# Scoring two steps of a narrow block in one pair of PSUM banks: steps 2 with 3 and 4 with 5 become pairs in a float32 decoder layer

## The chip, the cores and the metric

The kernel runs on one core of a Trainium2 chip, as one program. The metric is device time in microseconds (us). A profile is one execution of it, recorded by the hardware profiler; its times are read from the start of its span. TensorE is PE in the views (its weight loads PEld), VectorE is DVE, ScalarE is ACT, GpSimd is POOL and SyncE is SP.

## The reference: what is computed

One layer on x of 4 sequences x 512 tokens x 128 channels, all float32: causal self-attention with 16 heads of 8 channels and a learned relative bias, then cross-attention to 77 context tokens, then a mixture of 8 experts with one shared expert. Only the first part is touched, and the layer norm between the first and the second:

```
x = x + attn(_layernorm(x))
#   logits = where(j <= i, (q.k + q.rel_key[clip(j - i + 255, 0, 255)]) * scale, -inf)
#   out    = softmax(logits) @ v;   out @ Wo + bo
x = x + xattn(_layernorm(x), ctx)
#   q and k are normed once more inside each head
x = x + ffn(_layernorm(x))
```

## The kernel before, in words

Self-attention runs over the 4 sequences b, each in 4 blocks of 128 queries. `ORDER` is [2, 1, 3, 0]: the n-th block of a sequence is query block 2, 1, 3, 0. A block is numbered g = 4b + n, from 0 to 15. Query block 0 sees up to 128 keys and query block 1 up to 256: these are the narrow blocks (n = 3 and n = 1). Blocks 2 and 3 are the wide ones. A block has 8 steps u = 0 to 7 of 16 queries; s = 8g + u counts all 128 steps. A step's rows are 16 queries x 8 heads on 128 partitions, twice: `half` 0 and 1 are two sets of 8 heads in two PSUM banks. `psS` has four banks, and step s uses banks 2(s%2) and 2(s%2)+1.

Each engine's program is written out by hand in one loop over s, and engines meet only at semaphores:

- TensorE: `scores(s)` (L1403: q.k, 16 matmul instructions, and L1413: the relative part, 16 more), then `transpose_weights(s - 2)` (L1432: turns the softmax weights of the step before last), then at u = 2 to 5 `attend_block(g - 1, u - 2)` (L1372: a quarter of the previous block's weighted sum of values). Small things hang on certain steps: `sum_rows` at u = 4 (L1460), `project_o` at u = 7 (L1379), pieces for the cross-attention in the upper half of bank `psM` (`key_piece` L1480, `tokens_piece` L1488, `queries_piece` L1496, `heads_piece` L1504), and `early_probe` (L1513).
- VectorE: the negated maxima of the step's rows (L1058), then the copies of transposed weights of step s - 2 (`copy_units`, L1014), then a piece of a layer norm where there is one. At u = 2 `spread_sums` (L1020, L1021) and at u = 6 `finish` (L990) stand ahead of the maxima.
- ScalarE: some copies of step s - 2 (L625, wide blocks only), then two exponentials of step s (L663), then at u = 5 `copy_inverses` (L610), then the copy of a piece (L631 keys, L637 and L642 tokens and queries, L648 heads).
- GpSimd: `build_queries` makes the masked queries of a block (L479, L485) in one of two slots as soon as the block that used the slot has its scores; between them stand the root of a variance (L445) and `prepare` (L470).

The waits that matter: `scores(s)` waits until the exponentials of step s - 2 have read their banks; the exponentials of s wait for the maxima of s; `transpose_weights(s)` waits for the exponentials of s and, unit by unit, for the copy that empties its `psT` bank; a piece waits for the copy of the piece before it.

The layer norm of sequence f = b - 1 is spread over block n = 1 of the next sequence, as `ln_mean` (L850, L851) at u = 1, `ln_subtract` (L856) at u = 2, `ln_square` (L866) at u = 3, `ln_sum` (L875, L876) at u = 4, and at u = 5 `refine` (L834 to L836, after GpSimd's root) and `ln_multiply` (L888). `tokens_piece` at u = 6 waits for it. The head norm of the queries has its `head_sum` (L920, L921) at u = 7 of n = 2.

Of the kernel before, what the change touches and what calls it, by code (L numbers as in the profile page):

```python
# [60 lines left out]
def build(nc, x, ctx_in, pack_a, pack_b, rel_base, out):  # L61
# [6 lines left out]
    with ExitStack() as stack:  # L68
# [43 lines left out]
        neg_max = sb("neg_max", [128, 2, 2])  # L112
# [146 lines left out]

        def units(blk):  # L260


            return [list(range(j, min(j + 2, blk + 1))) for j in range(0, blk + 1, 2)]
# [62 lines left out]
        KEY_STEPS = (1, 3, 5, 6)  # L326
# [240 lines left out]
        def _(act):  # L567
# [83 lines left out]
            for s in range(ALL_STEPS):  # L651
                g, u = divmod(s, BS)
                b, n = divmod(g, TB)
                wide = width(ORDER[n], u)
                if s >= 2:
                    copy_units(s - 2)
                act.wait_ge(max_ready, s + 1)
# [4 lines left out]
                for half in range(2):  # L662
                    ins = nc.scalar.activation(prob[:, s % 4, half, 0:wide], psS[:, 2 * (s % 2) + half, 0:wide],  # L663
                                               ACT.Exp, bias=neg_max[:, s % 2, half:half + 1],
                                               accum_out=row_sum[:, g % 2, 2 * u + half:2 * u + half + 1])
                ins.then_inc(scores_read, 1)
                if g and u == 5:
# [136 lines left out]
        def _(dve):  # L804
# [240 lines left out]

            for s in range(ALL_STEPS):
                g, u = divmod(s, BS)
                wide = width(ORDER[g % TB], u)
# [6 lines left out]
                if g > 1 and u == 0:  # L1055
                    add_y(g - 2, tile_of(g - 2))
                dve.wait_ge(scores_ready, s + 1)
                v.tensor_reduce(neg_max[:, s % 2], psS[:, 2 * (s % 2):2 * (s % 2) + 2, 0:wide],  # L1058
                                AX_X, ALU.max, negate=True).then_inc(max_ready, 1)
                if s >= 2:  # L1060
                    copy_units(s - 2)
                if s == KEYS_AT:
# [261 lines left out]
        def _(pe):  # L1324
# [62 lines left out]
            def scores(s):  # L1387
# [4 lines left out]
                wide = width(blk, u)  # L1392
# [3 lines left out]
                pe.wait_ge(scores_read, PRO + s - 1)  # L1396


                for c in range(QG // QT):
                    q0 = QG * u + QT * c  # L1400
                    for half in range(2):
                        rows = slice(HALF_ROWS * half, HALF_ROWS * (half + 1))
                        mm(psS[32 * c:32 * c + 32, 2 * (s % 2) + half, 0:wide],  # L1403
# [3 lines left out]
                for c in range(QG // QT):  # L1407
# [493 lines left out]
```

## Time and profile before

| what | value |
|---|---|
| median of 3 runs | 498.47 us (497.95 to 498.8) |
| the profiled execution | 497.16 us, span 495.4 us |
| TensorE (PE) busy | 449.7 us, 91% of the span |
| VectorE (DVE) busy | 335.2 us, 68% |
| ScalarE (ACT) busy | 267.2 us, 54% |
| GpSimd (POOL) busy | 162.0 us, 33% |
| mean granted TensorE clock | 0.976 |
| the 128 steps of self-attention | 36.9 to 338.6 us |

The operations of VectorE in block 5, mean of one: maxima over 2x208 elements 0.59 us (L1058), over 2x160 0.49 us; copy of 512 elements 0.69 us and of 256 elements 0.41 us (L1014; two of 256 per step in query block 1, issued 0.33 us apart); L850, L856, L866, L875 and L888 0.67 to 0.69 us each; L851 and L876 0.17 us; L1020 0.25 us and L1021 0.42 us.

How to read it: busy time is a mean over stages, so what a change is worth is read in its own stretch. A matmul's end is modelled and reaches past the next one's start, so TensorE's phases are read from start to next start. "Idle before" names what released an instruction. PEclk is the granted clock, where 1.00 is 2.4 GHz and 0.50 is 1.2 GHz.

### The profile page before, as it was taken

To read this page: it belongs to the slowest core of one execution; us is meant where nothing else is said; L and a number is where in the kernel's file an instruction comes from. 1 tells how busy PE (TensorE), PEld (TensorE's weight loads), DVE (VectorE), ACT (ScalarE), POOL (GpSimd) and SP (SyncE) were. 2 spreads that over 40 slices of the span, in tenths; PEclk is the share of its full clock that TensorE was granted. 3 is DMA by queue.
4 is the path that set the end of the run, shared out by engine and by line. 5 is a ranking of instruction groups with operands and counts; after the bars stand their busy time and mean duration, and the time that the engine had idled before them with its cause. 6 is when DMAs were issued, how large, how long until landed. Compare 5 with 4: busy or idle time off the path is not lost.

```text
span 495.4 us, 17255 instructions
## 1 busy us (share of the span) xinstructions
PE 449.7 (91%) x7304; PEld 274.2 (55%) x7304; DVE 335.2 (68%) x684; ACT 267.2 (54%) x811; POOL 162.0 (33%) x95
## 2 busy tenths in 40 slices
PE   0879999999999799999799999998898989999997
PEld 0554655655655555655565665564454434666765
DVE  5555886657977667885857887766667587466633
ACT  2546556756456446556535655554454556554653
POOL 7147383333350952360752422084300000001000
PEclk9999999999999799999889999999889899999999
DMA  8211000000100000000000000000000004503151
GB/s 287 66 70 46 26 3 24 24 18 8 26 24 1 24 10 17 26 24 2 24 3 24 3 3 3 3 4 2 2 0 1 1 0 172 171 23 141 53 176 38
DMA packets 17465, 19.49 MB, mean 39 GB/s; under 512 B 1659, under 2 KB 14575, under 8 KB 17263
## 3 DMA queue, kind: packets, MB, share of 16 engines
q1 hardware_dynamic: 17391, 18.41, 11.5%
q8 instruction: 58, 0.95, 0.8%
q14 instruction: 16, 0.13, 0.1%
HBM read 16.17 MB, written 2.16 MB: 37 GB/s over the span
## 4 chain that ended last, share of the span: by engine, by line
PE 70%; DVE 17%; issue 5%; ACT 5%; DMA 2%; POOL 1%; DVEq 0%; SPq 0%; ACTq 0%; POOLq 0%
PE psT L1432 15%; PE psS L1403 14%; PE psS L1413 8%; PE psOM L1372 8%; PE psT L1792 5%; PE psS L1775 4%; DVE neg_max L1058 3%; DVE x_max L1033 2%; PE psS L1622 2%; PE psOM L1513 2%; ACT prob L663 2%; PE psT L1513 2%; PE psOM L1649 1%; DVE prob L1278 1%; PE psOM L1460 1%
## 5 line engine op out<-in xcount | busy, mean ns | idle before, releaser
L663 ACT ACTIVATE prob<-psS,neg_max 128x208 f32<-128x208 f32 (+23 forms) x256 | 121.2, 479 | 74.3 <-DVE neg_max L1058 74.1
L1058 DVE TENSOR_REDUCE neg_max<-psS 128x2 f32<-128x672 f32 (+23 forms) x128 | 91.7, 717 | 64.8 <-PE psS L1413 63.8
L445 POOL TENSOR_TENSOR stat<-stat,pack_a_sb 128x4 f32<-128x4 f32 (+2 forms) x16 | 54.7, 3416 | 169.9 <-DVE stat L876 123.0
L1432 PE MATMUL psT<-pack_a_sb,prob 128*128 128x128 f32 (+4 forms) x640 | 99.2, 287 | 6.3 <-DVE pt_even L1014 3.3
L1432 PEld LDWEIGHTS psT<-pack_a_sb,prob 128*128 128x128 f32 (+4 forms) x640 | 65.1, 133 | 48.5 <-issue 31.4
L1403 PE MATMUL psS<-k_v,q_both 64*32 64x336 f32 (+23 forms) x2048 | 88.5, 403 | 2.6 <-ACT prob L663 1.3
L1413 PE MATMUL psS<-rel_shifted,q_both 36*32 36x268 f32 (+16 forms) x2048 | 71.8, 338 | 0.0
L479 POOL TENSOR_TENSOR q_both<-qT,pack_a_sb 128x1024 f32<-128x1024 f32 x16 | 31.6, 1973 | 85.4 <-PE psS L1413 82.9
L1413 PEld LDWEIGHTS psS<-rel_shifted,q_both 36*32 36x32 f32 x2048 | 37.4, 110 | 24.7 <-issue 17.5
L663 ACT ACTIVATION_READ_ACCUMULATOR prob<-psS,neg_max 128x1 f32 x256 | 50.5, 197 | 0.0
L1792 PEld LDWEIGHTS psT<-pack_b_sb,prob 128*128 128x128 f32 x288 | 36.1, 191 | 18.6 <-DVE prob L1278 11.7
L1014 DVE COPY pt_even<-psT 128x512 f32<-128x512 f32 x64 | 43.6, 682 | 3.4 <-PE psT L1432 3.2
L713 ACT ACTIVATE prob<-psS 77x2048 f32<-77x2048 f32 x16 | 29.9, 1872 | 22.4 <-PE psS L1622 22.4
L1792 PE MATMUL psT<-pack_b_sb,prob 128*128 128x128 f32 x288 | 38.7, 278 | 3.6 <-DVE prob L1278 3.6
L485 POOL TENSOR_TENSOR q_both<-q_rep,pack_a_sb 128x1024 f32<-128x1024 f32 x16 | 41.1, 2568 | 0.0
L1403 PEld LDWEIGHTS psS<-k_v,q_both 64*32 64x32 f32 x2048 | 23.6, 106 | 25.3 <-issue 17.8
L1775 PE MATMUL psS<-qT,pack_b_sb 128*128 128x512 f32 x72 | 36.4, 594 | 0.0
L625 ACT ACTIVATE pt_diag<-psT 80x256 f32<-80x256 f32 (+2 forms) x64 | 23.9, 374 | 23.0 <-PE psT L1432 23.0
L625 ACT ACTIVATE pt_even<-psT 128x256 f32<-128x256 f32 x32 | 12.3, 383 | 33.4 <-PE psT L1432 33.4
L768 ACT ACTIVATE prob<-psS 128x512 f32<-128x512 f32 x36 | 21.2, 590 | 12.2 <-PE psS L1775 12.2
L1014 DVE COPY pt_diag<-psT 80x256 f32<-80x256 f32 (+2 forms) x64 | 26.3, 411 | 0.8 <-PE psT L1432 0.7
L1372 PE MATMUL psOM<-pt_diag,V_now 128*32 128x128 f32 x512 | 26.0, 280 | 0.0
(172 smaller groups left out, 597.7 us busy)
## 6 DMA issues: line engine op xcount, KB each, us to landing
q_rep<-q_scratch SPq DMA_DIRECT2D x128, 32.0 KB
k_v<-w_scratch SPq DMA_DIRECT2D x8, 512.0 KB, 5.9
q_both<-w_scratch SPq DMA_DIRECT2D x8, 512.0 KB, 6.6
pack_b_sb<-pack_b_dram SPq DMA_DIRECT2D x1, 1641.5 KB, 9.7
X<-x_dram SPq DMA_DIRECT2D x4, 256.0 KB, 5.3
q_scratch<-qT SPq DMA_DIRECT2D x4, 256.0 KB, 2.0
out_dram<-X SPq DMA_DIRECT2D x4, 256.0 KB, 2.3
pack_a_sb<-pack_a_dram SPq DMA_DIRECT2D x1, 535.0 KB, 4.4
```

The lines of the kernel that those rows point to most:

```text
L445: nc.gpsimd.tensor_tensor(st[:, 5, 0:groups], st[:, 2, 0:groups], ca["root"][0:parts, 0:groups], ALU.pow).then_inc(seeded, 1)
L485: nc.gpsimd.tensor_tensor(q_rel[:, slot].rearrange("p (g i) h -> p g i h", i=QT), q_rep[:, slot].rearrange("p h (g i) -> p g i h", i=QT), ...
L625: ins = nc.scalar.activation(dst, src, ACT.Copy)
L663: ins = nc.scalar.activation(prob[:, s % 4, half, 0:wide], psS[:, 2 * (s % 2) + half, 0:wide], ACT.Exp, bias=neg_max[:, s % 2, half:half + 1],
L1014: ins = v.tensor_copy(dst, src)
L1058: v.tensor_reduce(neg_max[:, s % 2], psS[:, 2 * (s % 2):2 * (s % 2) + 2, 0:wide], AX_X, ALU.max, negate=True).then_inc(max_ready, 1)
L1372: ins = mm(psO[quadrant * 32:quadrant * 32 + 32, 0:T], val, w, start=(i == 0 and n == 0), stop=(i == HQ - 1 and n == len(mine[0]) - 1))
L1403: mm(psS[32 * c:32 * c + 32, 2 * (s % 2) + half, 0:wide], q_blk[rows, g % 2, q0:q0 + QT, :].rearrange("p i h -> p (i h)"), kT[rows, b * S: ...
L1413: ins = mm(psS[32 * c:32 * c + 32, 2 * (s % 2) + half, lo:wide], q_rel[rows, g % 2, q0:q0 + QT, :].rearrange("p i h -> p (i h)"), rel[rows ...
L1432: ins = nc.tensor.transpose(psT[0:w, k % 2, at:at + T], prob[:, s % 4, half, j * T:j * T + w], ident)
L1775: mm(psS[:, k % 4, :], cb["w1"][:, e * D:e * D + D], xn_of[b], start=True, stop=True).then_inc(h_ready, 1)
L1792: ins = mm(psT[:, b % 2, t * D:t * D + D], hidden[:, k % 3, t * T:t * T + T], cb["w2"][:, e * D:e * D + D], start=(i == 0 and t == 0), sto ...
```

## The change

In the narrow blocks steps 2 and 3 and steps 4 and 5 are taken as pairs. Both steps of a pair write their scores into the same two banks, the first at column 0, the second at column 256. The pair of banks now alternates per fill and not per step. TensorE issues both scores, then both transposes, then both quarters of the previous block; VectorE takes the maxima of both steps in one instruction (over the wider of the two widths, so the scores of step 4 get 16 columns more) and then does the copies of both earlier steps. The exponentials stay one per step and half. `neg_max` has four slots.

The layer norm's parts in block n = 1 stand one step earlier each (0, 1, 2, 3), with the last at u = 5 as before. The four key pieces go from block 3 (u = 1, 3, 5, 6) to block 4 (u = 1, 2, 3, 6); only the last now waits for `rec_copied`.

```diff
+        def in_pair(g, u):
+            return ORDER[g % TB] < 2 and 2 <= u <= 5
+        def read_width(g, u):
+            return width(ORDER[g % TB], u | 1 if in_pair(g, u) else u)
+        def pair_of_banks():
+            fills, firsts = [], []
+            for s in range(ALL_STEPS):
+                g, u = divmod(s, BS)
+                if not (in_pair(g, u) and u % 2):
+                    firsts.append(s)
+                fills.append(len(firsts) - 1)
+            return fills, firsts
+        def bank_at(s):
+            g, u = divmod(s, BS)
+            return 2 * (fill_of[s] % 2), 256 * (u % 2) if in_pair(g, u) else 0
-        KEY_STEPS = (1, 3, 5, 6)
+        KEY_STEPS = (1, 2, 3, 6)
...
 # VectorE
+            def maxima_of_pair(s):
+                bank, at = bank_at(s)
+                dve.wait_ge(scores_ready, s + 2)
+                v.tensor_reduce(neg_max[:, s % 4:s % 4 + 2, :].rearrange("p s b -> p b s"),
+                                psS[:, bank:bank + 2, :].rearrange("p b (s j) -> p b s j", s=2)
+                                [:, :, :, 0:read_width(*divmod(s, BS))],
+                                AX_X, ALU.max, negate=True).then_inc(max_ready, 1)
...
+                if not in_pair(g, u):
+                    maxima(s)
+                    if s >= 2:
+                        copy_units(s - 2)
+                elif u % 2 == 0:
+                    maxima_of_pair(s)
                     copy_units(s - 2)
+                    copy_units(s - 1)
...
-                if f >= 0 and n == 1 and u == 1:
+                if f >= 0 and n == 1 and u == 0:
                     dve.wait_ge(y_added, (f + 1) * TB + ONE)
                     ln_mean(f)
+                if f >= 0 and n == 1 and u == 1:
+                    ln_subtract(f)
                 if f >= 0 and n == 1 and u == 2:
-                    ln_subtract(f)
+                    ln_square()
                 if f >= 0 and n == 1 and u == 3:
-                    ln_square()
-                if f >= 0 and n == 1 and u == 4:
                     ln_sum()
...
 # TensorE
-                pe.wait_ge(scores_read, PRO + s - 1)
+                if fill_of[s] > 1:
+                    pe.wait_ge(scores_read, PRO + first_step[fill_of[s] - 1])
...
-                scores(s)
-                if s >= 2:
+                if not in_pair(g, u):
+                    scores(s)
+                    if s >= 2:
+                        transpose_weights(s - 2)
+                    if g and 2 <= u <= 5:
+                        attend_block(g - 1, u - 2)
+                elif u % 2 == 0:
+                    scores(s)
+                    scores(s + 1)
                     transpose_weights(s - 2)
-                if g and 2 <= u <= 5:
+                    transpose_weights(s - 1)
+                else:
+                    attend_block(g - 1, u - 3)
                     attend_block(g - 1, u - 2)
-                if b == 0 and n == 3 and u in KEY_STEPS:
+                if g == TB and u in KEY_STEPS:
                     key_piece(KEY_STEPS.index(u), g)
```

## Rows read from the trace of the kernel before

**Rows 1.** Busy time by stretch: steps u = 2 to 5 of the eight narrow blocks

```profile
core 0: us, PE busy (x) PEld busy (x) DVE busy (x) ACT busy (x) POOL busy (x), PEclk, DMA share, GB/s
55.56:65.08 9.52, 9.48 (x246) 6.04 (x245) 8.23 (x19) 3.95 (x17) 2.21 (x2) 1.00 0.11 32
...
200.58:210.72 10.14, 10.14 (x249) 6.44 (x248) 8.60 (x21) 5.85 (x23) 2.04 (x3) 1.00 0.10 30
...
326.48:334.47 7.99, 7.63 (x270) 5.31 (x268) 4.01 (x11) 3.53 (x22) 7.37 (x1) 1.00 0.02 4
sum 74.02, PE 73.41 PEld 48.39 DVE 49.34 ACT 35.77 POOL 28.80; mean PE 9.18 PEld 6.05 DVE 6.17 ACT 4.47 POOL 3.60
```

**Rows 2.** TensorE in order of time, step 4 of block 5: start, us, engine, line

```profile
129.50 0.58 PE L1403 MATMUL psS<-k_v,q_both 64*32 64x208 f32 x16
...
130.36 0.66 PE L1432 MATMUL psT<-pack_a_sb,prob 128*128 128x128 f32 x4
130.95 0.64 PE L1372 MATMUL psOM<-pt_even,V_now 128*32 128x128 f32 x16
...
131.74 0.44 PE L1460 MATMUL psOM<-spread,pack_a_sb 128*64 128x128 f32 x4
```

**Rows 3.** TensorE in order of time, first two steps, nothing between them

```profile
37.38 0.68 PE L1413 MATMUL psS<-rel_shifted,q_both 36*32 36x272 f32 x16
37.84 0.70 PE L1403 MATMUL psS<-k_v,q_both 64*32 64x288 f32 x16
```

**Rows 4.** TensorE in order of time, step 5 of block 6

```profile
154.32 0.65 PE L1413 MATMUL psS<-rel_shifted,q_both 36*32 36x272 f32 x16
154.90 1.09 PE L1432 MATMUL psT<-pack_a_sb,prob 128*128 128x128 f32 x8
155.92 0.43 PE L1372 MATMUL psOM<-pt_odd,V_now 128*32 128x128 f32 x8
```

**Rows 5.** TensorE: 8 attend matmuls alone (block 4), 32 in one run (block 15)

```profile
114.47 0.42 PE L1372 MATMUL psOM<-pt_diag,V_now 128*32 128x128 f32 x8
...
339.64 1.08 PE L1372 MATMUL psOM<-pt_diag,V_now 128*32 128x128 f32 x32
```

**Rows 6.** TensorE in order of time, four instructions it idled before, in blocks 3, 5, 15

```profile
101.50 0.32 PE L1480 MATMUL psOM<-pack_a_sb,spaced 77*128 77x77 f32 x2 [0.21 <-ACT rec L610]
...
104.11 0.49 PE L1379 MATMUL psOM<-pack_b_sb,oT 128*128 128x128 f32 x2 [0.30 <-ACT khT L631]
...
136.58 0.41 PE L1488 MATMUL psOM<-pack_a_sb,stage 128*128 128x128 f32 x2 [0.54 <-DVE stage L888]
...
327.67 0.86 PE L1372 MATMUL psOM<-pt_even,V_now 128*32 128x128 f32 x24 [0.36 <-DVE x_max L1033]
```

**Rows 7.** GpSimd and VectorE in order of time, steps 0 and 1 of block 9

```profile
198.36 2.59 POOL L485 TENSOR_TENSOR q_both<-q_rep,pack_a_sb 128x1024 f32<-128x1024 f32 x1
...
199.73 0.49 DVE L1058 TENSOR_REDUCE neg_max<-psS 128x2 f32<-128x320 f32 x1 [0.30 <-PE psS L1413]
...
201.56 0.17 DVE L851 TENSOR_SCALAR stat<-stat 128x4 f32<-128x4 f32 x1
```

**Rows 8.** All engines in order of time, end of block 6 and start of block 7

```profile
162.58 2.55 POOL L485 TENSOR_TENSOR q_both<-q_rep,pack_a_sb 128x1024 f32<-128x1024 f32 x1
...
163.27 1.92 DVE L921 TENSOR_SCALAR stat<-stat 128x64 f32<-128x64 f32 x1
...
166.47 1.94 PE L1432 MATMUL psT<-pack_a_sb,prob 128*128 128x128 f32 x8 [2.32 <-ACT prob L663]
```

**Rows 9.** Busy time by stretch, columns of Rows 1: after the idle time of Rows 8

```profile
165.80:172.60 6.80, 6.13 (x108) 4.17 (x108) 2.93 (x8) 2.45 (x14) 6.80 (x1) 0.50 0.14 41
```

**Rows 10.** VectorE in order of time: maxima over 832 elements, in block 6

```profile
142.22 1.02 DVE L1058 TENSOR_REDUCE neg_max<-psS 128x2 f32<-128x832 f32 x1 [0.23 <-PE psS L1413]
```

**Rows 11.** ScalarE and TensorE in order of time, steps 2 and 3 of block 9

```profile
203.02 0.43 ACT L663 ACTIVATE prob<-psS,neg_max 128x208 f32<-128x208 f32 x1 [0.96 <-DVE neg_max L1058]
...
203.85 0.56 ACT L648 ACTIVATE x_qT<-psOM,pack_b_sb 128x256 f32<-128x256 f32 x1
...
205.44 0.44 PE L1504 MATMUL psOM<-pack_a_sb,spaced 128*128 128x128 f32 x2
```

More of the change, by code:

```diff
@@ L649, in copy_heads_tile, with exponentials @@
                                      ACT.Identity, scale=cb["ln_g"], bias=cb["q_b"]).then_inc(piece_read, 1)
-            for s in range(ALL_STEPS):
+            def exponentials(s):
                 g, u = divmod(s, BS)
-                b, n = divmod(g, TB)
-                wide = width(ORDER[n], u)
-                if s >= 2:
-                    copy_units(s - 2)
-                act.wait_ge(max_ready, s + 1)
+                wide = width(ORDER[g % TB], u)
+                bank, at = bank_at(s)
+                act.wait_ge(max_ready, fill_of[s] + 1)
                 if s >= 4:
@@ L662, in _ @@
                 for half in range(2):
-                    ins = nc.scalar.activation(prob[:, s % 4, half, 0:wide], psS[:, 2 * (s % 2) + half, 0:wide],
-                                               ACT.Exp, bias=neg_max[:, s % 2, half:half + 1],
+                    ins = nc.scalar.activation(prob[:, s % 4, half, 0:wide], psS[:, bank + half, at:at + wide],
+                                               ACT.Exp, bias=neg_max[:, s % 4, half:half + 1],
                                                accum_out=row_sum[:, g % 2, 2 * u + half:2 * u + half + 1])
                 ins.then_inc(scores_read, 1)
+            for s in range(ALL_STEPS):
+                g, u = divmod(s, BS)
+                b, n = divmod(g, TB)
+                if s >= 2:
+                    copy_units(s - 2)
+                exponentials(s)
                 if g and u == 5:
                     copy_inverses(g - 1)
-                if b == 0 and n == 3 and u in KEY_STEPS:
+                if g == TB and u in KEY_STEPS:
                     copy_keys(KEY_STEPS.index(u))
@@ L1391, in scores @@
                 blk = ORDER[n]
-                wide = width(blk, u)
+                wide = read_width(g, u)
+                bank, at = bank_at(s)
                 if u == 0:
@@ L1402, in scores @@
                         rows = slice(HALF_ROWS * half, HALF_ROWS * (half + 1))
-                        mm(psS[32 * c:32 * c + 32, 2 * (s % 2) + half, 0:wide],
+                        mm(psS[32 * c:32 * c + 32, bank + half, at:at + wide],
                            q_blk[rows, g % 2, q0:q0 + QT, :].rearrange("p i h -> p (i h)"),
@@ L1467, in pieces_until @@
                 steps = [divmod(k, BS) for k in range(g * BS + u)]
-                return sum(len(pieces_of(*k)) for k in steps) + sum(k[0] == 3 and k[1] in KEY_STEPS for k in steps)
+                return sum(len(pieces_of(*k)) for k in steps) + sum(k[0] == TB and k[1] in KEY_STEPS for k in steps)
             def key_piece(b, g):
@@ L1476, in key_piece @@
                 pe.wait_ge(piece_read, b)
-                if b > 1:
+                if b == B - 1:
                     pe.wait_ge(rec_copied, g)
@@ L1556, in _ @@
                 f = b - 1
-                if b == 0 and n == 3 and u in KEY_STEPS:
+                if g == TB and u in KEY_STEPS:
                     key_piece(KEY_STEPS.index(u), g)
```

19 lines of the change are left out of this document (11 added, 8 removed).

## The prediction, made before the changed kernel ran

> **What bounds the kernel now.** I read the busy table first (TensorE 91%), then busy time by stretch for exactly the steps that the change pairs, u = 2 to 5 of the eight narrow blocks [rows 1]. The reader is to see there that TensorE is busy for 73.41 of 74.02 us, and VectorE for only 49.34. So the maxima that are merged are not what these steps wait for, and a VectorE saving by itself is worth next to nothing. What counts is what TensorE's order costs it. That I read in order of time: one step of query block 1 is scores 0.86 us (129.50 to 130.36), transposes 0.59 and attend 0.79 (130.95 to 131.74) [rows 2], each kind of work followed by another kind. The waits that remain, and the three places where VectorE stands behind GpSimd, come from the same view [rows 6 to 8].
>
> **The change part by part.** Letters S, T, A are scores, transposes, attend; a pair goes from S T A S T A to S S T T A A.
>
> 1. *S next to S.* The last score group, 272 columns, holds TensorE 0.46 us when scores follow (37.38 to 37.84) [rows 3] and 0.58 us when transposes follow (154.32 to 154.90) [rows 4]. Saved 0.12 us a pair.
>
> 2. *T next to T.* Four transposes take 0.59 us [rows 2], eight in a run, over two banks, 1.02 (154.90 to 155.92) [rows 4]. Two fours made one eight save 2 x 0.59 - 1.02 = 0.16 in query block 1. The slope is (1.02 - 0.59)/4 = 0.11 per transpose, which leaves about 0.15 fixed per change of work, so block 0 (two per step) saves about as much. I take 0.15.
>
> 3. *A next to A.* Eight attend matmuls show 0.42 us, thirty-two in one run 1.08 [rows 5]: 0.0275 each, so 24 more add 0.66 where a separate 24 takes 0.79 [rows 2]. Saved 0.13.
>
> Together 0.40 us per pair, with TensorE bound there. Low end 0 (the changeover is only an effect of modelled ends, or something else holds TensorE), high end 0.5 where the clock is half. Against it stand 16 more columns in step 4: 16/208 of 0.86 is 0.07 at most; the part that doesn't grow with width taken out, 0.05. A narrow block so gains 2 x 0.40 - 0.05 = 0.75 us.
>
> The Trainium skill has a rule that speaks against item 2. "TensorE: Matmul & The Clock Gate", section "The mechanism", says that a weight load overlaps a running matmul only where the row groups differ; transposes use all rows, so each would pay its load wherever it stands and a longer run would save nothing. The run of eight at 1.02 against 2 x 0.59 disagrees, and I go by it; by the rule the sum would be 16 x 0.15 = 2.4 us less.
>
> 4. *Do the pairs wait?* The cover shrinks in one place: T of step 1 now comes right after S S T, without the attend between. In block 0 the chain is short and nothing is late. After S of step 3 come T T A A S S, about 1.0 + 1.4 + 1.6 = 4.0 us in block 1, against 1.02 for the maxima over 832 elements [rows 10] and 0.83 us per step of exponentials (203.02 to 203.85) [rows 11]: 2.7 us in all. Enough, if the maxima start in time. So blocks 1, 3, 7, 11 and 15, where no layer norm is on VectorE, get the full 0.75: 3.75 us. In block 1 the centring of the context keys stands before the second pair's maxima and takes some 3 us, but four phases of TensorE follow those maxima before it needs them. In 7 and 11 part of the work runs at half clock; that stretch ends by itself, so I count the same 0.75.
>
> 5. *The norm's parts in blocks 5, 9, 13.* `ln_mean` at u = 0 falls beside GpSimd's L485, which runs 198.36 to 200.95 [rows 7]. In the one place where a DVE tensor_scalar meets L485 now it takes 1.92 us instead of 0.2 and ends at 165.19, just after L485 at 165.13 [rows 8]. L851 is that operation. In block 9 it would be ready at about 200.1 (copy, then the 0.67 us reduce) and end at 201.0; queued behind it are the maxima of step 1, now at 199.73 [rows 7], 1.3 us late. Then copy 0.69, L856 0.67 and L1020 with L1021 0.67 put the pair's maxima at 203.4 to 204.4, the exponentials of step 2 at 205.3 and the copy of the heads piece (0.56, [rows 11]) at 205.9. TensorE, from 200.58: S S 1.6, T T 1.0, piece 0.3, A A 1.45 = 205.0, where the next piece waits for that copy: 0.9 us idle. So steps 2 to 5 go from 10.14 [rows 1] to 10.14 - 0.75 + 0.9 = 10.3, 0.15 worse. Given back: `ln_sum` and the root are a step earlier, and no maxima stand at u = 5, so stage is ready by about 211.9 where TensorE needs it at 212.4; before it idled there (0.54 in block 5 [rows 6]; some 0.35 by the same view in 9 and 13). Net +0.25 gained in block 9, the same in 13, where the probe's maximum is late as well and the idle time merely comes earlier. Block 5 has no heads pieces, so no idle time in the pairs; but VectorE then is the longer chain, stage is ready at about 135.8, the piece starts at 136.1 where it now starts at 136.58 [rows 6]: 0.5. Three blocks: 1.0 us. Bounds: L851 not blocked, up to 0.75 + 0.4 each, 3.4; blocked with full effect and nothing given back, -0.5.
>
> The rule behind it: "SBUF — State Buffer", section "Who interferes with whom", of the Trainium skill says that a tensor_scalar can enter a mode that takes the port pair shared with GpSimd, exclusively, and that whoever comes first holds it. The trace agrees (1.92 us). By the rule alone the block of L851 is sure; without it the sum would be 2.4 us larger.
>
> 6. *Key pieces.* Their two stalls in block 3 go, 0.21 and 0.30 [rows 6]. The pieces' own time moves to block 4, equal. What is late there: `project_o` waits for the last key copy, about level with TensorE. I charge 0.15. Net 0.35, between 0 and 0.5.
>
> 7. *Block 15.* The attend that waits 0.36 us for the probe's maximum [rows 6] moves behind a second S and T, 0.8 us: 0.35 gained.
>
> 8. *The merged maxima* save some 0.1 us of VectorE each; TensorE hides that, 0.
>
> Sum: 3.75 + 1.0 + 0.35 + 0.35 = 5.45 us. The profiled execution took 497.16 (span 495.4), so 491.7; the median of the runs shown stands 1.3 above it at 498.47, so **493.0 us**.
>
> **The rivals.**
>
> *A, the clock falls (slower).* Where TensorE idled 2.32 us [rows 8], with 0.8 just before it, the granted clock went to 0.50 for 6.8 us [rows 9], which costs up to 3.4 us. If the new 0.9 us of idle time in blocks 5, 9 and 13, caused by L851 behind L485, do the same, each costs about 3.2. From two falls on the 5.45 are gone; three make 498.5 - 5.45 + 9.6 = 502.6. Against it: idle times of 0.4 to 0.8 us stand in many places at 1.00.
>
> *B, no changeover saved.* S T A keep their price in any order, and only the waits go: 0.35 + 0.35 + about 0.8 = 1.5, so 497.0. For it: ends are modelled. Against it: items 1 to 3 are from start to start.
>
> *C, VectorE's late start holds every block of n = 1,* also 1 and 5, and takes the changeovers there: 5.45 - 2.5 = 2.95, so 495.5. Busy 8.60 of 10.14 us [rows 1] speaks for it.
>
> *D, L851 is too small to be held.* Blocks 5, 9, 13 give 3.4 instead of 1.0: 490.6.
>
> *E, the pairs change nothing that counts:* 498.5.
>
> **How the numbers follow.** Within 0.2% (1.0 us either way, about what can be told from no change) is 497.5 to 499.5. Chances: forecast 0.55 (491.3 to 495), A 0.11, B 0.13, C 0.09, D 0.08, E 0.04. Faster is forecast, C, D and most of B, 0.83; same is E and the rest of B, 0.07; slower 0.10. The range from 490.5 to 497.3 takes in D, C and B and leaves A and E out.
>
> **What would show it.** Right: S S T T A A in the narrow blocks, u = 2 to 5 of blocks 3 and 15 about 0.75 us shorter apart from the waits; L851 at 0.8 to 0.9 us in block 9, ending with L485; idle time before the second heads piece of some 0.9 us; none before L1488 in block 9; clock 1.00 there. Wrong: changeovers as long as now in the pairs, T of step 1 waiting for exponentials, or a granted clock of 0.50 in blocks 5, 9 or 13.

## The result, and the profile after

The changed kernel takes 490.57 us (median of 4 runs, 488.51 to 491.75) against 498.43 us (4 runs). The ratio is 0.9839, 95% interval [0.9804, 0.9873], so 7.9 us less. The forecast was 5.45 us less (493.0, range 490.5 to 497.3), so the result stands at the range's low end, and by the ratio, 490.4, just under it. In a second series of six executions the same kernel gave 488.93 against 497.37, ratio 0.9816 [0.9781, 0.985].

The profiled execution took 488.51 us with a span of 486.7, against 497.16 and 495.4. The page of the kernel after: busy time by engine, then the group of the maxima that are left one by one (96 of 128; the 16 merged ones are L1093).

```profile
PE 440.3 (90%) x7304; PEld 276.1 (57%) x7304; DVE 333.7 (69%) x668; ACT 265.6 (55%) x811; POOL 162.1 (33%) x95
...
L1086 DVE TENSOR_REDUCE neg_max<-psS 128x2 f32<-128x672 f32 (+9 forms) x96 | 77.0, 802 | 43.1 <-PE psS L1470 42.3
```

TensorE is busy for 9.4 us less, VectorE for 1.5. The number of matmuls is the same (7304): what went is time at the changes from one kind of work to another and, as the experiments show, time at half clock. The stretches of [rows 1] in the kernel after (same columns; blocks 1, 3, 5, 7, 9, 11, 13, 15):

```profile
55.59:64.16 8.57, 8.57 (x246) 6.61 (x245) 7.66 (x16) 2.91 (x14) 1.72 (x2) 1.00 0.13 35
92.95:100.25 7.30, 7.18 (x269) 5.67 (x268) 3.36 (x9) 4.08 (x23) 0.06 (x1) 1.00 0.15 40
123.39:132.23 8.84, 8.60 (x246) 6.61 (x245) 8.67 (x19) 3.98 (x18) 2.49 (x3) 1.00 0.13 37
165.36:173.24 7.88, 7.88 (x269) 6.21 (x268) 3.01 (x8) 4.07 (x23) 7.88 (x1) 0.85 0.07 19
196.12:206.33 10.21, 9.23 (x249) 7.06 (x248) 9.07 (x21) 5.80 (x23) 2.60 (x3) 1.00 0.11 30
242.47:251.03 8.56, 8.56 (x270) 6.77 (x269) 3.77 (x9) 2.88 (x17) 5.92 (x1) 0.78 0.02 5
277.73:287.00 9.27, 9.19 (x250) 7.06 (x249) 8.16 (x19) 5.53 (x22) 2.25 (x2) 1.00 0.02 5
320.40:327.41 7.01, 7.01 (x270) 5.75 (x268) 3.65 (x9) 3.45 (x22) 7.01 (x1) 1.00 0.03 7
sum 67.64, PE 66.23 PEld 51.73 DVE 47.35 ACT 32.69 POOL 29.94; mean PE 8.28 PEld 6.47 DVE 5.92 ACT 4.09 POOL 3.74
```

The sum is 67.64 where it was 74.02. TensorE in order of time over the second pair of block 5, which answers to [rows 2]; matmuls of each kind stand together:

```profile
127.71 0.61 PE L1460 MATMUL psS<-k_v,q_both 64*32 64x224 f32 x16
...
129.39 1.09 PE L1489 MATMUL psT<-pack_a_sb,prob 128*128 128x128 f32 x8
130.41 0.44 PE L1517 MATMUL psOM<-spread,pack_a_sb 128*64 128x128 f32 x4
```

From start to next start, with both steps added up:

| steps 4 and 5 of block 5 | before | after |
|---|---|---|
| scores | 0.87 + 0.92 | 1.68 |
| transposes | 0.59 + 0.58 | 1.02 |
| sums | 0.37 | 0.37 |
| attend | 0.79 + 0.79 | 1.45 |
| together | 4.91 | 4.52 |

Block by block, self-attention changed by (us, first profiles): block 1 -0.33; block 3 -1.89 and block 4 +0.75 (the key pieces moved); block 5 -1.13; block 7 -1.88; block 9 -0.57; block 11 -0.56; block 13 -0.50; block 15 -0.97; other wide blocks 0.00. That is 7.1. The last 1.6 us are in a part whose code is unchanged, everything after the last block (called the tail below): 156.77 us before, 155.18 after.

### The profile page after: what moved, and what is told of

The parts are those of the page before. It is cut to its first block, busy times and chain, and to the rows that moved or that the text cites. A ratio compares the mean times of both kernels' runs of the same rounds, so it can differ in the third digit from the quotient of the medians.

```text
span 486.7 us, 17235 instructions
## 1 busy us (share of the span) xinstructions
PE 440.3 (90%) x7304; PEld 276.1 (57%) x7304; DVE 333.7 (69%) x668; ACT 265.6 (55%) x811; POOL 162.1 (33%) x95
## 3 DMA queue, kind: packets, MB, share of 16 engines
q1 hardware_dynamic: 17391, 18.41, 11.2%
## 4 chain that ended last, share of the span: by engine, by line
PE 67%; DVE 18%; issue 5%; ACT 5%; DMA 3%; POOL 1%; SPq 0%; DVEq 0%; ACTq 0%; POOLq 0%
PE psT L1489 15%; PE psS L1460 13%; PE psS L1470 8%; PE psOM L1426 7%; PE psT L1859 5%; PE psS L1842 4%; DVE neg_max L1086 2%; DVE x_max L1069 2%; ACT prob L692 2%; PE psOM L1570 2%; PE psS L1689 2%; DMA q_both<-w_scratch 2%; PE psT L1570 2%; DVE pt_even L1050 2%; PE psOM L1716 1%
## 5 line engine op out<-in xcount | busy, mean ns | idle before, releaser
L475 POOL TENSOR_TENSOR stat<-stat,pack_a_sb 128x4 f32<-128x4 f32 (+2 forms) x16 | 54.7, 3417 | 163.3 <-DVE stat L912 116.9
L1086 DVE TENSOR_REDUCE neg_max<-psS 128x2 f32<-128x672 f32 (+9 forms) x96 | 77.0, 802 | 43.1 <-PE psS L1470 42.3
L1489 PE MATMUL psT<-pack_a_sb,prob 128*128 128x128 f32 (+4 forms) x640 | 95.9, 285 | 6.6 <-DVE pt_even L1050 3.5
L515 POOL TENSOR_TENSOR q_both<-q_rep,pack_a_sb 128x1024 f32<-128x1024 f32 x16 | 41.0, 2565 | 0.0
L1460 PEld LDWEIGHTS psS<-k_v,q_both 64*32 64x32 f32 x2048 | 26.1, 106 | 22.7 <-issue 15.8
```

What stands on the lines that cost most here:

```text
L475: nc.gpsimd.tensor_tensor(st[:, 5, 0:groups], st[:, 2, 0:groups], ca["root"][0:parts, 0:groups], ALU.pow).then_inc(seeded, 1)
L515: nc.gpsimd.tensor_tensor(q_rel[:, slot].rearrange("p (g i) h -> p g i h", i=QT), q_rep[:, slot].rearrange("p h (g i) -> p g i h", i=QT), ...
L1086: v.tensor_reduce(neg_max[:, s % 4], psS[:, bank:bank + 2, 0:read_width(*divmod(s, BS))], AX_X, ALU.max, negate=True).then_inc(max_ready, 1)
L1460: mm(psS[32 * c:32 * c + 32, bank + half, at:at + wide], q_blk[rows, g % 2, q0:q0 + QT, :].rearrange("p i h -> p (i h)"), kT[rows, b * S:b ...
L1489: ins = nc.tensor.transpose(psT[0:w, k % 2, at:at + T], prob[:, s % 4, half, j * T:j * T + w], ident)
```

## The experiments

All kernels are variants of the kernel after unless said otherwise; times are medians, ratios stand against the kernel before in the same series. The code in the cuts is shortened.

**The same kernels again**

Nothing is edited in e1, e15 and e16.

> The changed kernel once more, unaltered. Theory 1 (the surplus over the forecast 5.45 us is granted clock: in the changed kernel's first profile the clock fell to 0.50 for 3.4 us in block 7 where it was 6.8 before, and one fall fewer came after self-attention): another execution has falls of other lengths at the same idle times, so the profiled span differs by 1 to 3 us from 486.7 while the blocks at clock 1.00 repeat to 0.05 us. Rival (the surplus is work that I costed too low): the span repeats within 0.5 us and so do the falls. Median 490 to 491.

> The kernel before, unaltered, one more profiled execution. Theory (the part of the result beyond the blocks' own gains is how the granted clock fell in that one execution): blocks at clock 1.00 repeat to 0.03 us, and the span differs from the first profile's 495.4 by 0.5 to 3 us only in the places where the clock falls (block 7, block 11 and the tail), each fall costing 1.7 or 3.4 us. Rival: the falls come at the same places for the same lengths, and the span repeats to 0.5 us.

> The kernel after, unaltered, a third profiled execution. Same theory: blocks at clock 1.00 as in the first two profiles to 0.03 us, with steps 0 and 1 and 2 and 3 of block 7 between 10.4 and 11.4 us in sum by whether the fall there lasts 3.4 or 6.8 us, and the span between 486.5 and 489. Rival: a place other than block 7, block 11 and the tail differs by more than 0.1 us.

Spans: e1 488.6 and e16 486.9 us, where the first profile of the kernel after had 486.7; e15 495.9 where the first of before had 495.4. All blocks outside 7 and 11 repeat to 0.03 us (block 4 of before to 0.11). What differs is where the granted clock fell. That e15's span comes within 0.5 us of the first is two differences that cancel: 1.6 us more in the loading phase, 1.1 us less in block 7. Busy time by stretch, kernel before again (e15): steps 0 to 3 of blocks 7 and 11, and everything after the last block:

```profile
163.17:174.06 10.89, 7.76 (x213) 5.46 (x212) 7.20 (x15) 5.75 (x26) 10.70 (x3) 0.84 0.10 27
239.62:253.01 13.39, 10.74 (x229) 7.93 (x229) 8.68 (x17) 5.78 (x26) 13.20 (x3) 0.75 0.08 22
339.05:495.80 156.75, 141.06 (x979) 84.60 (x978) 95.52 (x216) 81.74 (x116) 12.16 (x13) 0.97 0.18 62
```

The same stretches of the kernel after again (e16):

```profile
159.13:169.57 10.44, 7.32 (x214) 5.65 (x213) 7.15 (x14) 5.70 (x26) 10.25 (x3) 0.84 0.10 28
234.28:247.36 13.08, 10.42 (x229) 8.19 (x228) 8.66 (x16) 5.69 (x26) 12.89 (x3) 0.74 0.08 23
331.66:486.90 155.24, 139.78 (x979) 83.72 (x978) 95.50 (x216) 81.79 (x116) 12.16 (x13) 0.97 0.19 62
```

The first of them took 12.04 us in the first profile of before and 10.43 in that of after: a gain of 1.61 there and 0.45 here, from the same edit. In the tail the kernel before shows three falls to 0.50 in both profiles, and here are those of e15:

```profile
350.50:353.90 3.40, 3.40 (x16) 1.78 (x16) 2.31 (x5) 0.00 (x0) 0.77 (x1) 0.50 0.00 0
367.60:371.00 3.40, 3.40 (x19) 1.81 (x20) 3.08 (x7) 0.45 (x1) 0.00 (x0) 0.50 0.00 0
391.50:394.90 3.40, 3.40 (x16) 1.48 (x17) 0.00 (x0) 1.93 (x2) 0.00 (x0) 0.50 0.00 0
```

and the kernel after two (e16):

```profile
359.10:362.50 3.40, 3.40 (x20) 1.70 (x16) 3.08 (x8) 0.72 (x1) 0.00 (x0) 0.50 0.01 2
383.00:386.40 3.40, 3.40 (x16) 1.48 (x15) 0.00 (x0) 2.12 (x2) 0.00 (x0) 0.50 0.02 5
```

e1 also shows two, at 343.5 and 367.4, and a tail of 155.97. Laid over the kernel after, start by start, the tail of before is 1.25 us behind once the fall at 350.1 is over, a fall that the kernel after hasn't got there, and it loses another 0.35 us near 426 us, where no fall stands in either profile; the cause of that part is open. So 1.25 of the 1.6 us go with one fall of the clock. Beyond what was expected, a fall can stand in the loading phase too: in e15 at 26.3 us, and the first block then starts at 38.54 instead of 36.92. Where the falls come is not a property of the kernel alone. So spans are best read against the granted clock that each execution reports:

| mean granted clock | before, span (executions) | after, span (executions) |
|---|---|---|
| 0.976 | 495.2 to 496.8 (24) | |
| 0.979 | 494.5 to 495.1 (9) | 488.3 to 490.0 (4) |
| 0.981 to 0.983 | 493.6 to 493.9 (5) | 486.7 to 487.5 (4) |

At the same clock the change is worth 5.8 us (means 494.7 and 488.9 at 0.979), and by the last row, where the clock of after is a little the lower, 6.7 (493.7 and 487.0). The median clock went from 0.976 (57 executions) to 0.981 (11), and 43 of the 57 executions of before are at 0.976 or lower where none of the 11 of after is. So the higher clock comes back with the kernel after, though no run shows what in the change brings it. From 0.976 to 0.983 the kernel before itself gets 2.1 us shorter (means), so 1.5 for the 0.005. The two parts come to 7.3 to 8.2, where 7.9 was measured.

**One part of the change at a time**

e2 keeps the pairs, with the norm and the key pieces where they were before; e4 keeps pairs and key pieces; e3 has no pairs.

```diff
# e2 and e4 (e2 also has KEY_STEPS and their block as before)
-                if f >= 0 and n == 1 and u == 0:
+                if f >= 0 and n == 1 and u == 1:
                     ln_mean(f)
...
-                if f >= 0 and n == 1 and u == 3:
+                if f >= 0 and n == 1 and u == 4:
                     ln_sum()
# e3
-            return ORDER[g % TB] < 2 and 2 <= u <= 5
+            return False
```

> The pairs alone; the norm's parts at steps 1 to 4 and the key pieces in block 3 as before. Changeover theory: u = 2 to 5 shorter by 0.7 to 0.9 us in blocks 1, 3, 7, 11, 15 apart from waits, so about 4 us, plus what blocks 5, 9, 13 give: with no tensor_scalar behind L515 there is no 0.97 us of idle time before the second heads piece, but tokens come later. Ratio to before 0.986 to 0.990 (4.5 to 7 us). Rival (VectorE's order, not TensorE's, brought the gain): within 1.5 us of before.

> The norm's parts one step earlier and the key pieces in block 4, no pairs. Changeover theory: the key stalls 0.35 us and at most the 1.2 us of stalls before tokens_piece go, so 0.5 to 1.5 us faster than before. Rival (moving the norm is what brought the gain): 3 us or more.

> Pairs and key pieces as changed, the norm's parts at steps 1 to 4 as before. My step 5 says that the tensor_scalar at u = 0 costs blocks 9 and 13 about 0.9 us of idle time, and that the earlier variance gives 0.6 to 0.9 back before tokens_piece: this kernel then is within 1 us of the changed one, with the 0.97 us idle gone and an idle time before tokens_piece in its place. Rival (the earlier norm is a clear gain): 1.5 us or more slower than the changed kernel.

Columns 4 to 6 are the change of a block against before, in us.

| | time | ratio | block 5 | block 9 | block 13 |
|---|---|---|---|---|---|
| e2 | 503.08 | 1.0107 [1.0071, 1.0143] | +2.78 | +2.12 | +2.89 |
| e3 | 497.11 | 0.9977 [0.9946, 1.0008] | +0.18 | +0.31 | +0.45 |
| e4 | 502.79 | 1.0074 [1.0036, 1.0112] | +1.47 | +3.24 | +2.68 |

e4's executions spread from 497.0 to 505.0 us; its row leaves out the three longest, and its blocks are from the longest, so what follows rests on e2. The expectations were missed: the pairs alone had been expected to bring nearly all of the gain, and e4 to come within 1 us of the kernel after, and both kernels are slower than the one before. In blocks 1 and 15 the pairs gain what they gain in the kernel after (0.32 and 0.97 us); what they lose in 5, 9 and 13 is more. VectorE, GpSimd and TensorE in order of time, e2, end of block 5:

```profile
130.07 1.09 DVE L1093 TENSOR_REDUCE neg_max<-psS 128x4 f32<-128x896 f32 x1 [0.28 <-PE psS L1470]
...
132.41 0.67 DVE L911 TENSOR_REDUCE stat<-sq 128x4 f32<-128x512 f32 x1
...
133.11 0.17 DVE L912 TENSOR_SCALAR stat<-stat 128x4 f32<-128x4 f32 x1
...
133.36 1.02 POOL L475 TENSOR_TENSOR stat<-stat,pack_a_sb 128x4 f32<-128x4 f32 x1 [8.67 <-DVE stat L912]
...
134.34 1.27 POOL L500 TENSOR_TENSOR X<-X,pack_b_sb 128x512 f32<-128x512 f32 x1
...
134.41 1.22 DVE L870 SCALAR_TENSOR_TENSOR stat<-stat 128x4 f32<-128x4 f32 x1 [1.13 <-POOL stat L475]
...
137.01 0.61 PE L1545 MATMUL psOM<-pack_a_sb,stage 128*128 128x128 f32 x2 [2.71 <-DVE stage L924]
```

The merged maxima and four copies stand as one piece of 2.3 us ahead of the sum. The sum, the root (L475) and then `refine` (L870, held until L500 ends) are late, and TensorE idles 2.71 us. Right behind that the granted clock is at half speed, in this block and the same way in 9 (from 215.6) and 13 (from 300.9):

```profile
137.10:140.50 3.40, 3.40 (x39) 1.83 (x40) 1.76 (x4) 1.43 (x6) 0.84 (x1) 0.50 0.00 0
```

So rival A's outcome (idle time, then half clock, slower than before) is real here, and the norm's earlier steps keep the change out of it. Norm and key pieces gain nothing that can be told from the spread when they are alone (e3, 0.5 to 1.5 us expected): blocks 3 and 4 together get 0.7 to 0.8 us shorter by the key pieces, but blocks 5, 9 and 13 lose 0.94. Without pairs the transposes of block 5 wait 0.94 us for a copy that stands behind `ln_mean` (held by L515) and `ln_subtract`, and steps 2 and 3 go from 4.49 to 5.47 us.

**Which part of the norm's move the pairs need**

```diff
# e11: start as before, sum one step earlier
+                if f >= 0 and n == 1 and u == 1:
                     ln_mean(f)
+                if f >= 0 and n == 1 and u == 2:
                     ln_subtract(f)
                 if f >= 0 and n == 1 and u == 3:
+                    ln_square()
                     ln_sum()
# e7: reduction at u = 0, its scaling (L887) at u = 1
                 if f >= 0 and n == 1 and u == 0:
-                    ln_mean(f)
+                    reduce_sum(stat[:, 0, 0:TB], xt)
...
                 if f >= 0 and n == 1 and u == 1:
+                    tensor_scalar(stat[:, 4, 0:TB], stat[:, 0, 0:TB], 1.0 / D)
                     ln_subtract(f)
```

> The pairs and key pieces as changed, the norm's mean at u = 1 and its subtraction at u = 2 as before, but square and sum both at u = 3, ahead of the second pair's maxima. Theory from e2 (with pairs, a sum at u = 4 comes only after the merged maxima and four copies, the root lands beside GpSimd's prepare L500 which holds L870 for 1.2 us, and TensorE idles 2.7 us at tokens_piece): here the sum is in time, that idle time is under 0.8 us in blocks 5, 9, 13, the clock does not fall there, no tensor_scalar meets L515, and the time is 487 to 491. Rival (what the norm needed was its early start at u = 0): 4 us or more slower than the changed kernel.

> The changed kernel with ln_mean's reduce left at u = 0 and its tensor_scalar moved to u = 1, where GpSimd's L515 is over. Port theory (the tensor_scalar is held until L515 ends, and behind it the maxima of step 1): the 0.9 us instruction takes 0.17, the idle time of 0.97 us before the second heads piece in block 9 falls under 0.2, the 0.9 us in u = 0 to 1 of block 13 goes; blocks 9 and 13 each 0.6 to 0.9 us shorter, block 5 0 to 0.3. Rival (the late maxima come from VectorE's amount of work): no change.

e11: 489.85 us, 0.9849 [0.9808, 0.9889]; blocks 5, 9 and 13 are 0.22, 0.94 and 0.91 us shorter than in the kernel after. So the pairs need the sum to stand ahead of the second pair's maxima, not the early start. e7: 489.16 us, 0.9809 [0.9764, 0.9854]; the same blocks are 0.70, 0.73 and 0.72 shorter. GpSimd and VectorE, kernel after, steps 0 and 1 of block 9, which answer to [rows 7]:

```profile
193.90 2.58 POOL L515 TENSOR_TENSOR q_both<-q_rep,pack_a_sb 128x1024 f32<-128x1024 f32 x1
...
195.60 0.90 DVE L887 TENSOR_SCALAR stat<-stat 128x4 f32<-128x4 f32 x1
196.53 0.49 DVE L1086 TENSOR_REDUCE neg_max<-psS 128x2 f32<-128x320 f32 x1
...
201.47 0.30 PE L1561 MATMUL psOM<-pack_a_sb,spaced 128*128 128x128 f32 x1 [0.97 <-ACT x_qT L678]
```

L887 starts at 195.60 and ends at 196.50, with L515 at 196.48. It is 0.90 us instead of 0.17, and TensorE idles 0.97 us before the second piece, where 0.9 was forecast. Moved away from L515 (e7) it costs 0.7 us a block less, in block 5 too, where 0 to 0.3 had been expected. The medians of e7 and e11 hardly show their 2.1 us: blocks 7 and 11 are 0.9 and 1.0 us longer in e7 at a lower granted clock (0.974 for the execution, e11 0.972, after 0.982).

**The order of the pair, and the merged maxima**

```diff
# e6: S S T A T A
                     transpose_weights(s - 2)
-                    transpose_weights(s - 1)
+                    attend_block(g - 1, u - 2)
                 else:
-                    attend_block(g - 1, u - 3)
+                    transpose_weights(s - 2)
                     attend_block(g - 1, u - 2)
# e5: two maxima for a pair
-                v.tensor_reduce(neg_max[:, s % 4:s % 4 + 2, :]...
+                for i in range(2):
+                    v.tensor_reduce(neg_max[:, (s + i) % 4], psS[:, bank:bank + 2, 256 * i:...
```

> The changed kernel with TensorE's order S S T A T A in a pair in place of S S T T A A; banks, maxima and norm as changed. Changeover theory: each of the 16 pairs pays one more T to A and A to T, 0.15 + 0.13 us by my items 2 and 3, so u = 2 to 5 of a narrow block are 0.5 to 0.6 us longer (block 15: 7.02 to about 7.6) and the whole some 4 us slower where TensorE is the bound. Rival (only the score changeover is real, the rest is an effect of modelled ends): under 1 us slower.

> The changed kernel with two maxima per pair, one for each step, both after the second step's scores, in place of the merged one. Changeover theory (TensorE's changes of work bring the gain; the merged maxima save 0.1 us of VectorE each, hidden): blocks 3, 7, 11, 15 the same to 0.05 us; blocks 1, 5, 9, 13, where VectorE is the longer chain, at most 0.3 us longer each; in all 0 to 1.2 us slower than the changed kernel. Rival (VectorE's saved instruction brings the gain): 4 us or more slower.

e6: 494.75 us, 0.9929 [0.9896, 0.9963]; each pair of block 15 costs 0.26 and 0.27 us more than after, each of block 1 0.28 and 0.29. The forecast for T T and A A together was 0.28. TensorE in order of time, e6, one pair of block 15, transposes and attend:

```profile
330.87 0.42 PE L1489 MATMUL psT<-pack_a_sb,prob 128*80 128x128 f32 x2
331.21 0.86 PE L1426 MATMUL psOM<-pt_even,V_now 128*32 128x128 f32 x24
331.89 0.40 PE L1426 MATMUL psOM<-pt_diag,V_now 128*32 128x128 f32 x8
332.23 0.44 PE L1517 MATMUL psOM<-spread,pack_a_sb 128*64 128x128 f32 x4
332.60 0.41 PE L1489 MATMUL psT<-pack_a_sb,prob 128*80 128x128 f32 x2
```

The two transposes take 0.34 us from start to next start; in the kernel after the four together take 0.57 (324.59 to 325.16), and 64 attend matmuls 1.88 (325.53 to 327.41) instead of 2 x 1.01. e5: 490.52 us, 0.9846 [0.98, 0.9892]; blocks 1, 5, 9 and 13 are 0.06 to 0.13 us longer, block 7 about 0.18, blocks 3, 11 and 15 equal. The merged maxima are worth some 0.5 us in all; they are not where the gain is.

**What the half clock of blocks 7 and 11 costs**

```diff
# e10 (and e9, the same in the kernel before); e8 has u == 2; block 14 stays as it was
                 if f >= 0 and n == 2 and u == 7:
-                    head_sum(sq_flat, stat, TB * H)
+                    reduce_sum(stat[:, 1, 0:TB * H], heads(sq_flat))
+                if f >= 0 and n == 3 and u == 1:
+                    tensor_scalar(stat[:, 2, 0:TB * H], stat[:, 1, 0:TB * H], 1.0 / HD, EPS)
```

> The changed kernel with head_sum's tensor_scalar (and so its root) moved from u = 7 of block 6 and 10 to u = 2 of block 7 and 11, past GpSimd's L515. Clock theory (what costs blocks 7 and 11 most is this one instruction held 1.9 us, TensorE's idle time behind it, and the half clock that follows): u = 0 to 1 of block 7 go from 6.3 or more to about 3.4 us and of block 11 from about 8 to about 5.1, the granted clock stays 1.00 in both, u = 2 to 3 fall to about 3.6 and 3.3; in all 6 to 9 us faster than the changed kernel, about 481. Rival (the idle time comes from the copies of transposed weights and returns in another place): within 2 us.

> The kernel before, with head_sum's tensor_scalar (and so its root) moved from u = 7 of blocks 6 and 10 to u = 1 of blocks 7 and 11, behind that step's copies and past GpSimd's L485. Clock theory: the idle times of 2.3 and 1.9 us at the start of blocks 7 and 11 go, the clock stays 1.00 there, and blocks 7 and 11 become about 13.5 and 16.5 us (now 18.1 and 20.4); 7 to 9 us faster than before in the profiled span, about 490 us. Rival: it was chance that this tensor_scalar met L485, and another wait takes its place: within 3 us.

> The changed kernel with the same move as e9. Against e9 it shows what the pairs and the norm are worth with no fall of the clock in self-attention: by the blocks at clock 1.00 (blocks 1, 3 with 4, 5, 7, 9, 11, 13, 15) 6.0 to 6.6 us, of which my sum named 5.45. Rival (the surplus over 5.45 us is not clock but stays with the pairs): 8 us or more. Block 12, where the later root made GpSimd late in e8 (1.3 us), within 0.3 of the changed kernel.

| block times in us | time | ratio | block 7 | block 11 | clock (profile) |
|---|---|---|---|---|---|
| e9 against before | 487.14 | 0.9798 [0.9766, 0.983] | -4.6 | -4.6 | 0.986 |
| e10 against after | 484.61 | 0.9745 [0.9713, 0.9777] | -2.85 | -4.26 | 0.993 |
| e8 against after | 486.06 | 0.9756 [0.9718, 0.9794] | -2.57 | -4.60 | 0.989 |

The operation that [rows 8] shows held for 1.92 us (there L921) is the cause of the 2.32 us of idle time and of the half clock behind it in both kernels. Taken out from beside L515, both go, and the granted clock of blocks 7 and 11 is 1.00. With them gone the change itself is worth less: from e9 to e10 block 7 gains 0.1, block 11 0.2 and block 15 0.5 us, self-attention as a whole 4.2, where 6.0 to 6.6 had been expected. The medians differ by 2.5, with e9's executions at clocks of 0.986 to 0.996 and e10's at 0.979 to 0.993. In e10 runs of 64 attend matmuls take 2.04 and 2.21 us in some blocks instead of 1.88, with no releaser in the trace; that is about 1 us of the miss, and why stays open. e8 missed the 481 us expected of it as well: its blocks 7 and 11 came as expected, but block 12 and the tail took 1.3 and 2.7 us back. A later root has a price of its own. VectorE and GpSimd in order of time, e8, around step 2 of block 12:

```profile
249.93 1.96 POOL L509 TENSOR_TENSOR q_both<-qT,pack_a_sb 128x1024 f32<-128x1024 f32 x1
251.85 2.57 POOL L515 TENSOR_TENSOR q_both<-q_rep,pack_a_sb 128x1024 f32<-128x1024 f32 x1
...
252.44 2.27 DVE L1057 TENSOR_TENSOR spread<-row_inv,pack_a_sb 128x256 f32<-128x256 f32 x1
```

L515 now covers the step in which `spread_sums` stands, and its L1057 takes 2.27 us instead of 0.42; the steps 2 and 3 of that block are 1.30 us longer. In e10 the same happens in block 8 (L1057 2.24 us, the block 1.03 us longer), and in block 8 of e9 (the same operation 2.15 us, the block 0.94 us longer). The Trainium skill, "SBUF — State Buffer", section "Who interferes with whom", says that a VectorE instruction with two SBUF inputs contends with a GpSimd instruction that reads SBUF. The trace agrees (2.27 us), and so looking out for tensor_scalar alone is too narrow when something is moved.

**Versions that combine the gains**

e12: e7's and e10's edits, and the centring of the context keys of block 1 (one piece of 3 us, see below) spread over steps 4 to 7. e13: e7's and e10's edits. e14: e13 with that centring at steps 5, 6, 7 and its sum at 10.

```diff
# e14 (e12: KEYS_AT = 4 and the sum at KEYS_AT + 3)
-        KEYS_AT = 11
+        KEYS_AT = 5
-                    head_centre(ctx_k[:], xc_flat[0:M], sq_flat[0:M], stat[0:M], M, TB * H)
+                    head_mean(ctx_k[:], stat[0:M], TB * H)
+                if s == KEYS_AT + 1:
+                    head_subtract(...)
+                if s == KEYS_AT + 2:
+                    head_square(...)
+                if s == KEYS_AT + 5:
+                    head_sum(...)
```

> A version meant to beat both: the changed kernel with e7's split mean, with the context keys' head_centre spread over steps 4 to 7 of block 0 in place of one piece at step 11 (block 1's 0.6 us at u = 6 to 7 goes), and with e9's later head_sum. By blocks: 0.6 in block 1, 0.7 each in 5, 9, 13, about 3 in block 7 and 4.5 in block 11 against the changed kernel's first profile; 479 to 482 us. Rival (VectorE is then the bound and gives part back): 484 or more.

> The kernel after, with the reduction of ln_mean kept at u = 0 of blocks 5, 9 and 13 and its tensor_scalar moved to u = 1 (as in e7), and in blocks 7 and 11 the tensor_scalar of head_sum moved to u = 1 (as in e10). The two edits lie in different blocks, so theory: the gains add. Blocks 5, 9, 13 0.70, 0.73 and 0.72 us shorter than after (e7), block 7 and 11 about 2.4 to 2.9 and 4.3 to 4.6 shorter (e10), block 8 about 1.0 longer (e10): e10's 484.6 less 2.1 gives 482.5. Block 1 as in after (about 12.9 us by its steps), since the centring that e12 had spread stays where after has it. Rival: the shorter blocks bring the clock down somewhere else, a half-clock stretch of 3.4 us costing 1.7 or a longer one 3.4; then 484 to 486 although each named block measures as said.

> As e13_best3, and the centring of the context keys in block 1 taken apart: its mean at step 5, its subtraction at step 6, its square at step 7, its sum at step 10, where e12 had the sum at step 7 behind a GpSimd operation. Theory: what block 1 lost in steps 6 and 7 (4.02 us instead of 3.40 before) was the 3 us of VectorE work in one piece ahead of the second pair's maxima; then steps 6 and 7 come to 3.4 to 3.6 and the kernel is 0.4 to 0.6 us under e13. Rival: the centring is late for the heads that are projected from it at the end of block 1 or the start of block 2, or its parts stand in front of the first pair's copies; then block 1 or 2 is 0.5 to 3 us longer.

e12 missed: 487.62 us, 0.9792 [0.9763, 0.9821], with block 1 3.79 us longer than after. Its sum's scaling met L515 (order of time, e12):

```profile
56.15 2.18 DVE L957 TENSOR_SCALAR stat<-stat 77x64 f32<-77x64 f32 x1
...
59.67 0.85 PE L1503 MATMUL psT<-pack_a_sb,prob 128*128 128x128 f32 x6 [2.45 <-DVE pt_even L1050]
```

e13: **482.62 us**, 0.9687 [0.9641, 0.9733]; 482.5 was expected. Blocks 5, 9 and 13 are 0.70, 0.73 and 0.72 us shorter than after, as expected. Block 7 gains 2.07 (2.4 to 2.9 expected) and block 11 4.38, block 8 loses 0.25 (1.0 expected); the tail is 157.9 us with a stretch of 6.8 us at half clock. The gains add, and part of them goes to the clock. e14: **482.08 us**, 0.9662 [0.9614, 0.971], the best kernel here, though not told apart from e13. Its steps 6 and 7 of block 1 come back to 3.40 us, as expected, but steps 0 and 1 lose 0.67 us, as its rival said. VectorE and TensorE in order of time, e14, around step 0 of block 1:

```profile
53.50 0.87 DVE L952 TENSOR_TENSOR sq<-xc 77x512 f32<-77x512 f32 x1
...
53.73 0.85 PE L1503 MATMUL psT<-pack_a_sb,prob 128*128 128x128 f32 x6 [0.69 <-DVE pt_even L1050]
...
55.60 0.85 PE L1503 MATMUL psT<-pack_a_sb,prob 128*128 128x128 f32 x6 [0.32 <-DVE pt_even L1050]
```

The square puts the copies of both steps behind it; the same two transposes waited 0.37 and 0 us after.

## Why the prediction was right and wrong

*Items 1 to 3, the changes of work (0.12, 0.15, 0.13): right in query block 1, too high in query block 0.* In block 5's second pair the scores gain 0.11 net of the wider step, transposes 0.15, attend 0.13, together 0.39 us; in the second pair of blocks 7, 11 and 15 0.27. There the sixteen more columns eat nearly all of what S next to S saves (0.94 to 0.92 us), which the prediction put at 0.05 everywhere. Experiment e6 confirms T T and A A by themselves (0.26 to 0.29 a pair, 0.28 forecast). Rivals B and E fall with it: a change of work costs real time.

*Item 4, blocks 1, 3, 7, 11, 15 (3.75): too high in block 1.* The step that failed reads: "four phases of TensorE follow those maxima before it needs them". VectorE in order of time, kernel after, block 1:

```profile
59.61 0.66 DVE L942 TENSOR_REDUCE stat<-ctx_k 77x64 f32<-77x512 f32 x1
...
62.69 0.19 DVE L957 TENSOR_SCALAR stat<-stat 77x64 f32<-77x64 f32 x1
63.03 1.09 DVE L1093 TENSOR_REDUCE neg_max<-psS 128x4 f32<-128x896 f32 x1
```

The maxima start at 63.03 although their scores were there a microsecond and more before, the exponentials of both steps at 64.16, so steps 6 and 7 take 4.02 us instead of 3.40. The block gains 0.33, not 0.75. What the centring delayed was behind the pairs, in steps 6 and 7.

*Item 5, blocks 5, 9, 13 (1.0): mechanism right, size short.* L887 was held (0.92, 0.90 and 0.89 us), the idle time before the second piece was 0.97, steps 2 to 5 of block 9 are 0.07 us longer (0.15 forecast). So rival D falls as a mechanism; that its 490.6 is the time measured is chance. But the three blocks give 2.20 us, 1.2 more than the sum had. Given back was more than I took, above all in block 5 (1.13 instead of 0.5). VectorE there, kernel after:

```profile
131.15 0.41 DVE L1050 COPY pt_odd<-psT 128x256 f32<-128x256 f32 x1
...
132.47 0.15 DVE L870 SCALAR_TENSOR_TENSOR stat<-stat 128x4 f32<-128x4 f32 x1
...
133.05 0.69 DVE L924 TENSOR_TENSOR stage<-xc,stat 128x512 f32<-128x512 f32 x1
```

Stage is ready 10.3 us after step 2 started (VectorE's next start, 133.66, less 123.39); the forecast had 10.8, before it was 11.2. The half microsecond is L870: 0.15 us here, 0.79 before, where it stood beside `prepare`. The prediction moved the root one step ahead, but not the operations that it frees from `prepare`. Rival C (VectorE holds the n = 1 blocks) falls for the second pair, whose 4.52 us are TensorE's own time; in the first pair of block 5 TensorE does wait 0.24 us for a copy, and steps 2 and 3 gain only 0.17.

*Item 6, key pieces (0.35): the total is right by luck.* Blocks 3 and 4 together gain 1.0 to 1.15, forecast 0.75 + 0.35. But the key pieces alone give 0.7 to 0.8 (e3) and the pairs alone 0.5 to 0.6 (e2): one term too small, the other too large. *Item 7, block 15 (0.35):* the idle time of 0.36 is gone, the block gains 0.97 of 1.10. *Item 8, merged maxima (0):* some 0.5.

*The step that failed, and made the sum too small,* is the one on the clock: "that stretch ends by itself, so I count the same 0.75", and no term at all for the part after the blocks. What was gained, by pairs of profiles (us):

| | forecast | after against before | e16 against e15 | e1 against before |
|---|---|---|---|---|
| blocks other than 7 and 11 | 3.95 | 4.66 | 4.52 | 4.63 |
| blocks 7 and 11 | 1.50 | 2.44 | 1.31 | 1.47 |
| after the blocks | 0 | 1.59 | 1.58 | 0.80 |

The first row is item 5's 1.2 us too little, less block 1's 0.4 and small differences. The second hangs on the falls: where block 7 has one of 3.4 us after and of 6.8 us before, the two blocks give 2.44; where both kernels have falls of equal length (e16 and e15, e1 and before), about the 1.5 forecast; and with no fall at all (e9 to e10) 0.3, or 0.8 without the slow attend runs of e10, so 0.75 a block is not their gain at full clock. The third is a term that the sum put at nothing, and 1.25 us of the 1.6 are the fall of the clock that the kernel after hasn't got in two of its three profiles. Of these five profiles only e15 has a fall in the loading phase, another 1.6 us. So the time came to the low end of the range by two things the sum hadn't: the norm's chain (1.2 us) and the granted clock (about 1.5 us by the medians, 0.976 to 0.981). What moves the falls in the tail wasn't found; that the change caused their number to drop isn't shown. Rival A didn't come: the new idle time of 0.97 us stayed at 1.00. The prediction looked for it in the wrong place: the fall comes when the pairs are made without the norm's move (e2), a question that the prediction never asked.

## What to carry to other kernels

Price a change of TensorE's order by the start-to-start times of runs of each length: here a change of kind costs 0.1 to 0.15 us, and it added up over 16 pairs. Before grouping work on one engine, ask what small operation behind the group feeds a long chain (here the norm's sum), and move that ahead first; it decided the sign. Compare executions at the same granted clock, and ask for each small VectorE operation which GpSimd operation it will stand beside: two of them, 0.2 us each when free, cost the kernel before 10 us (e9), idle time and half clock behind them included.

## What the runs showed of the hardware

In self-attention, idle times of TensorE of 1.9 to 2.8 us were followed by a granted clock of 0.50 for 3.4 to 10.2 us (10.2 in block 11 of e2, e3, e6, e7 and e11, behind 1.9 us of idle time); those of 0.97 us (after) and 1.26 us (e8) were not. The length of the idle time doesn't decide alone: in the tail of before falls stand behind 0.90 and 1.08 us (at 367.2 and 391.1), and none behind 1.00 us at 403.9. The length of the half-clock stretch differs between executions of one kernel (block 7: 3.4 or 6.8 us), and so does whether one stands in the loading phase, worth 1.6 us. A tensor_scalar on 128x4 elements waits for a running GpSimd tensor_tensor (0.90 us instead of 0.17), a scalar_tensor_tensor (1.22 instead of 0.15) and a two-input tensor_tensor (2.27 instead of 0.42) too; reductions and PSUM copies beside the same L515 kept theirs (0.68 and 0.69 us).
